# The entry of a two-layer graph kernel: weights' maxima, first norm and weight splits in another order

## What is computed

```python
h = relu(layernorm(x))                                   # 256 x 512
q, k, v = heads(h @ Wq + bq), heads(h @ Wk + bk), heads(h @ Wv + bv)   # 16 heads of 32
attn = softmax(where(adj == 0, -inf, q @ k.T / sqrt(32)))
x = x + (attn @ v) @ Wo + bo
h = relu(layernorm(x))
alpha = relu((h @ wq1) @ (h @ wk1).T) * (adj != 0)
x = x + softmax(alpha, axis=1) @ (h @ weight)
```

## Time and profile before

| | us |
|---|---|
| median of 3 runs | 1569.24 (1568.12 to 1569.25) |
| the profiled execution's own time | 1570.8 |
| its span in the trace | 1569.0 |
| mean granted TensorE clock in it | 0.992 of full |

### The profile page before, as it was taken

The page is one execution under the profiler, slowest core; times in us unless marked ns, Lnnn a source line. Parts: engine busy times, 40 slices in busy tenths (PEclk is TensorE's granted clock), DMA queues, the critical chain, the costliest instruction groups (busy, mean ns, idle before and its releaser), DMA issues.

```text
span 1569.0 us, 50846 instructions
## 1 busy us (share of the span) xinstructions
PE 1504.6 (96%) x16561; PEld 1106.7 (71%) x16561; DVE 1247.9 (80%) x4042; ACT 1128.3 (72%) x2477; POOL 1064.8 (68%) x1478
## 2 busy tenths in 40 slices
PE   2889999999999999999999999999999999999996
PEld 1557777777777777777777777777777777777753
DVE  6778888887887878788888878888887888888763
ACT  2567777777777777777777777777777777777761
POOL 2466767777677777767677776777776777777650
PEclk9999999999999999999999999999999999999998
DMA  7647777667667766666776766777676677767760
GB/s 241 135 95 132 133 163 160 152 136 152 138 138 166 160 144 143 144 136 148 166 157 141 152 140 134 154 160 159 135 158 136 133 161 160 153 135 159 125 119 16
DMA packets 656198, 226.28 MB, mean 144 GB/s; under 512 B 611488, under 2 KB 627872, under 8 KB 656160
## 3 DMA queue, kind: packets, MB, share of 16 engines
q1 hardware_dynamic: 636848, 188.57, 59.1%
q10 hardware_dynamic: 19312, 37.23, 8.5%
HBM read 57.94 MB, written 16.78 MB: 48 GB/s over the span
## 4 chain that ended last, share of the span: by engine, by line
POOL 35%; issue 34%; PE 22%; DVE 4%; ACT 2%; DMA 1%; POOLq 1%; SPq 0%; ACTq 0%; DVEq 0%
PE ring L408 18%; POOL wv_raw L1115 16%; POOL heads_out L1149 6%; POOL x L1172 4%; POOL keep L1181 3%; POOL far L1190 3%; POOL xa L1137 1%; PE score L464 1%; PE pv L483 1%; DMA turned<-wv_raw 1%; POOL newton L1133 1%; PE ring L518 1%; PE pv L485 0%; DVE wk_raw L864 0%; DVE tops L785 0%
## 5 line engine op out<-in xcount | busy, mean ns | idle before, releaser
L1115 POOL TENSOR_TENSOR wv_raw<-wk_raw,wv_raw 128x512 f16<-128x512 f32 x512 | 608.0, 1190 | 362.8 <-ACT wv_raw L638 358.5
L625 ACT ACTIVATE wk_raw<-wk_raw,least 128x256 f32<-128x256 f32 x1024 | 459.0, 497 | 6.8 <-DVE least L864 6.8
L864 DVE CUSTOM_DVE_ANT_0 wk_raw<-score,far,undo_score 128x256 f32<-128x256 f32 x1024 | 444.0, 478 | 7.1 <-issue 5.1
L638 ACT ACTIVATE wv_raw<-wk_raw 128x512 f16<-128x512 f32 x512 | 320.5, 626 | 8.6 <-issue 4.5
L483 PEld LDWEIGHTS pv<-val,turned 128*128 128x128 f16 x2048 | 149.7, 97 | 67.4 <-issue 43.9
L483 PE MATMUL pv<-val,turned 128*128 128x65 f16 x2048 | 185.9, 192 | 10.8 <-DMA turned<-wv_raw 7.0
L408 PE MATMUL ring<-wv_hi,h 128*128 128x256 f16 x1024 | 189.3, 273 | 0.0
L408 PE MATMUL ring<-h,wq_hi 128*128 128x256 f16 x1024 | 176.3, 274 | 7.6 <-DVE wk_lo L827 7.6
L1149 POOL TENSOR_TENSOR heads_out<-o_sum,o_rcp 128x64 f32<-128x64 f32 x512 | 153.0, 320 | 42.6 <-DVE o_sum L879 42.6
L485 PE MATMUL pv<-val,turned 128*128 128x33 f16 x2048 | 178.1, 179 | 0.0
L408 PE MATMUL ring<-h,wk_hi 128*128 128x256 f16 x1024 | 176.6, 274 | 0.0
(11 more groups left out here) (151 smaller groups left out, 3570.6 us busy)
## 6 DMA issues: line engine op xcount, KB each, us to landing
xin<-x_dram ACTq DMA_DIRECT2D x32, 512.0 KB, 3.8
out_dram<-xo SPq DMA_DIRECT2D x32, 512.0 KB, 3.7
xa<-x_dram ACTq DMA_DIRECT2D x31, 512.0 KB, 4.2
adj_in<-adj_dram SPq DMA_DIRECT2D x32, 256.0 KB, 2.9
turned<-wv_raw SPq DMA_TRANSPOSE x512, 3.2
adjt_in<-adj_t_dram SPq DMA_DIRECT2D x32, 256.0 KB, 3.1
wq_raw<-wq_dram SPq DMA_DIRECT2D x2, 512.0 KB, 7.0
wk_raw<-wk_dram SPq DMA_DIRECT2D x2, 512.0 KB, 8.6
```

The lines of the kernel that those rows point to most:

```text
L625: last = nc.scalar.activation(probs[:, at, q, :], probs[:, at, q, :], ACT.Exp, bias=least[:, at, q:q + 1], scale=-1.0)
L638: nc.scalar.activation(halves[:, at, :, 0, :], probs[:, at, :, :], ACT.Copy).then_inc(hi["p"], 1)
L864: last = nc.vector.tensor_tensor_reduce(out=probs[:, at, q, :], in0=score[u % GROUP][:, q * NODES:(q + 1) * NODES], in1=far[:, q, :], scal ...
L1115: nc.gpsimd.tensor_tensor(halves[:, at, :, 1, :], probs[:, at, :, :], halves[:, at, :, 0, :], ALU.subtract).then_inc(lo["p"], 1)
```

## The change

- **Loads.** SP issues wq right behind xa, then the biases, then wv; ACT's queue issues wk at the program's start.
- **Graph 0's norm.** VectorE does the refinement and the normalisation in place of POOL (three small instructions and two large ones in place of six and two).
- **Maxima first.** VectorE takes wq's and wk's maxima directly behind the low half of h, and the constants after them. `scaled` is raised as soon as the scales are there; `undo_score` and the two biases come behind it, with a semaphore of their own (`bias_ok`).
- **PE's start.** The first half of qk0 waits for wq's splits only. Eight float32 products of the identity with itself follow the first scale's products.
- **Values' scale.** Its rounding moves behind qk0's low half, its spreading behind graph 0's first scores.
- **Graph 1's norm.** Statistics in steps 12 and 13 of body(-1), root in 14, normalisation on POOL in 15, high half on ACT in step 1 of body 0, low halves in steps 2 and 3.
- **The nine jobs of body 0.** The spare places are now: h2_0 turn (scales of wo and w1), h2_1 merge 0, g0 spread, g1 merge 1, hw0 merge 2, al merge 3, hw1 turn (wm's scale), av0 spread, av1 bias product. ACT copies a merged tile out of its bank (`merged_copy`), VectorE takes the maximum of the copy. wo's maxima stand in step 15 of body(-1), w1's in steps 3 and 4 of body 0.
- **Splits.** wo in steps 8 and 9 of body 0, w1 in 10 and 11, wm in step 15 and in step 1 of body 1.

The code of bodies 2 and later is the same.

```diff
 STATS1, ROOT1, NORM1, LATE_MASK = (8, 9), 10, 12, 5
 XA_STEP, SCALE_STEP = 5, 6
+STATS1_FIRST, ROOT1_FIRST, NORM1_FIRST, HIGH1_FIRST, LOW1_FIRST = (12, 13), 14, 15, 1, (2, 3)
 HIGH1_STEP, LOW1_STEPS, TURN1_STEP = 14, (0, 2), 6
 VAR2 = 4
...
+JOBS = {"h2_0": "turn", "h2_1": 0, "g0": "spread", "g1": 1, "hw0": 2, "al": 3, "hw1": "turn",
+        "av0": "spread", "av1": "bias"}
+SPARE = [tile(name) for name in ORDER if tile(name) in JOBS]
+MERGES = [0, 1, 2, 3, "bias"]
+WARM = 8
...
-SPLIT_TURN = ("wq", "wk", "wv", "wo", "wm", "w1")
-TOP_STEP = 5
-LAST_SCALE_STEP = step_of(SPARE[-1])
-
-
-SPLIT_AT = {(0, 14): 6, (0, 15): 7, (1, 2): 8, (1, 3): 9, (1, 6): 10, (1, 7): 11}
-assert len(SPARE) == KT + 2 and TOP_STEP + 4 < LAST_SCALE_STEP
+TOP_AT = {(-1, 15): (("wo", 0), ("wo", 1)), (0, 3): (("w1", 0),), (0, 4): (("w1", 1),)}
+
+
+SPLIT_AT = {(0, 8): 6, (0, 9): 7, (0, 10): 8, (0, 11): 9, (0, 15): 10, (1, 1): 11}
...
             sp.dma_start(xa[:], x_v[0, :, :, :]).then_inc(xa_in, 16)
+            for half in range(2):
+                load_raw(sp, "wq", half)
             sp.dma_start(bias_q[:], bq).then_inc(small_in, 16)
             sp.dma_start(bias_k[:], bk).then_inc(small_in, 16)
             sp.dma_start(bias_v[:], bv).then_inc(small_in, 16)
             sp.dma_start(out_bias[:], bo.broadcast_to([P, DIM])).then_inc(small_in, 16)
-            for name in LOADS[:EARLY // 2]:
-                for half in range(2):
-                    load_raw(sp, name, half)
+            for half in range(2):
+                load_raw(sp, "wv", half)
...
+                dst, job = ring[BANK[SPARE[at]]], JOBS[SPARE[at]]
...
+                batch = 2 if at < 3 else 3
+                if job == "turn":
+                    turn_tops(batch, dst)
                     return
-                if at < KT:
-                    cols = slice(at * P, (at + 1) * P)
+                if job == "spread":
+                    spread_scale(batch, 2 if batch == 2 else 1, dst)
+                    return
...
-            WEIGHTS_BY = {("qk0", 0): (w_low, 4), ("v0", 0): (w_low, 6), ("wo0", 0): (w_low, 8),
-                          ("g0", 0): (w_low, 10), ("hw0", 0): (w_low, 12)}
+            WEIGHTS_BY = {("qk0a", 0): (w_low, 2), ("qk0b", 0): (w_low, 4), ("v0a", 0): (w_low, 6),
+                          ("wo0a", 0): (w_low, 8), ("g0", 0): (w_low, 12)}
...
@@ -594,16 +601,19 @@
                     if nxt and not cur and s == SCALE_STEP:
                         turn_tops(0, pv)
                         spread_scale(0, 2, pv)
-                    if nxt and not cur and s == step_of("qk0") - 1:
+                        for _ in range(WARM):
+                            nc.tensor.matmul(ring[1][:, 0:P], ident[:], ident[:], start=True,
+                                             stop=True)
+                    if nxt and not cur and s == step_of("qk0"):
                         turn_tops(1, pv)
-                    if nxt and not cur and s == step_of("qk0"):
-                        spread_scale(1, 1, pv)
                     if s in SCORE_STEPS:
                         g = SCORE_STEPS.index(s)
                         if g < 2 and nxt:
                             scores(g, t + 1)
                         elif g >= 2 and cur:
                             scores(g, t)
+                    if nxt and not cur and s == SCORE_STEPS[0]:
+                        spread_scale(1, 1, pv)
...
+            def merged_copy(name):
+                act.wait_ge(merged, MERGES.index(JOBS[name]) + 1)
+                nc.scalar.activation(raw["wm"][:, JOBS[name], :], ring[BANK[name]][:], ACT.Copy
+                                     ).then_inc(copied, 1)
...
+                    if isinstance(b, int) and b == 0 and k == 0:
+                        act.wait_ge(bias_ok, 1)
                     if k >= 2 or started(b - 1):
...
-                    if s == ROOT1 and later:
+                    if s == (ROOT1 if cur else ROOT1_FIRST) and later:
...
+                        elif cur and not prev and isinstance(JOBS.get(tile(name)), int) and not name.endswith("a"):
+                            merged_copy(tile(name))
...
-                    if nxt and not cur and s == step_of("qk0"):
+                    if nxt and not cur and s == SCORE_STEPS[0]:
                         act.wait_ge(scaled, 2)
                         for c in range(FIRST, EARLY):
                             split_high(c)
-                    if cur and not prev and s == LAST_SCALE_STEP:
-                        act.wait_ge(scaled, 3)
                     if cur and isinstance(t, int) and (t, s) in SPLIT_AT:
+                        act.wait_ge(scaled, 3 if SPLIT_AT[t, s] < 10 else 4)
                         split_high(SPLIT_AT[t, s])
-                    if s == HIGH1_STEP and later:
+                    if s == HIGH1_STEP and cur and later:
                         first_high(n + 1)
+                    if s == HIGH1_FIRST and cur and not prev:
+                        first_high(n)
                     if s == XA_STEP and later:
                         act.wait_ge(lo["h1"], count(n, QT, QT - 1))
                         act.dma_start(xa[:], x_v[n + 1, :, :, :]).then_inc(xa_in, 16)
+            for half in range(2):
+                load_raw(act, "wk", half)
...
-                src = ring[BANK[SPARE[at]]][:]
-                if at > KT:
-                    step(nc.vector.tensor_reduce(tops[:, 2, 0:1], most_merged[:], AX.X, ALU.max))
-                    find_scale(2, 3, 3, ring[BANK[SPARE[at]]])
+                bank, job = ring[BANK[SPARE[at]]], JOBS[SPARE[at]]
+                batch = 2 if at < 3 else 3
+                if job == "turn":
+                    round_tops(batch, 2 if batch == 2 else 1, bank)
                     nc.vector.sem_inc(merged_out, 1)
+                elif job == "spread" and batch == 2:
+                    take_scale(2, 3, 2, bank)
+                    nc.vector.sem_inc(merged_out, 1)
+                    nc.vector.sem_inc(scaled, 1)
                     step(nc.vector.tensor_tensor(undo_out[:], undo[:, 2:3], undo[:, 3:4],
                                                  ALU.mult))
                     step(nc.vector.tensor_scalar(undo_final[:], undo[:, 4:5], 1.0 / E_LIFT, None,
                                                  ALU.mult))
+                elif job == "spread":
+                    take_scale(3, 5, 1, bank)
+                    nc.vector.sem_inc(merged_out, 1)
                     nc.vector.sem_inc(scaled, 1)
-                    return
-                dve.wait_ge(merged, at + 1)
-                if at < KT:
-                    step(nc.vector.tensor_copy(raw["wm"][:, at, :], src))
-                    nc.vector.tensor_reduce(most_merged[:, at:at + 1], src, AX.X, ALU.max,
-                                            apply_absolute_value=True).then_inc(merged_out, 1)
+                elif job == "bias":
+                    dve.wait_ge(merged, MERGES.index(job) + 1)
+                    nc.vector.tensor_tensor(out_bias[:], bank[:], out_bias[:], ALU.add
+                                            ).then_inc(merged_out, 1)
                 else:
-                    nc.vector.tensor_tensor(out_bias[:], src, out_bias[:], ALU.add
-                                            ).then_inc(merged_out, 1)
+                    dve.wait_ge(copied, job + 1)
+                    step(nc.vector.tensor_reduce(most_merged[:, job:job + 1], raw["wm"][:, job, :],
+                                                 AX.X, ALU.max, apply_absolute_value=True))
+                    nc.vector.sem_inc(merged_out, 1)
+                    if job == KT - 1:
+                        step(nc.vector.tensor_reduce(top[:, 0:1], most_merged[:], AX.X, ALU.max))
+                        nc.vector.sem_inc(top_ok, 1)
...
+                    stats_at = STATS1 if cur else STATS1_FIRST
+                    if s in stats_at and later:
+                        first_stats(stats_at.index(s), n + 1)
+                    low_at = LOW1_STEPS if prev else LOW1_FIRST
+                    if s == low_at[0] and cur and nxt:
                         first_low(0, n)
+                    if isinstance(t, int) and (t, s) in TOP_AT:
+                        for name, half in TOP_AT[t, s]:
+                            raw_top(name, half, ("wo", "w1").index(name))
+                    if cur and not prev and s == 4:
+                        gather_tops(2)
...
-                    if nxt and not cur and s == step_of("qk0") - 1:
+                    if nxt and not cur and s == step_of("qk0"):
                         round_tops(1, 1, pv)
-                    if nxt and not cur and s == step_of("qk0"):
+                    if nxt and not cur and s == SCORE_STEPS[0]:
                         take_scale(1, 2, 1, pv)
                         nc.vector.sem_inc(scaled, 1)
...
+            y, a, c = rstd[0][:], newton[0][:, 1, :], newton[0][:, 2, :]
+            dve.wait_ge(rooted[0], 1)
```

(21 more changed lines are left out.)

47 lines of the change are left out of this document (18 added, 29 removed).

## The result

| | before | after |
|---|---|---|
| median, 8 runs each | 1567.78 (1566.38 to 1572.12) | 1571.53 (1570.33 to 1575.88) |
| ratio, with its 95% interval | | 1.0027 (1.0015 to 1.0039) |
| the profiled execution | 1570.8, span 1569.0 | 1571.63, span 1569.8 |

The changed kernel is slower, by 0.27%, where 0.4% faster was forecast. Its median lies 4.0 us above the upper end of the predicted range. The two profiled executions stand only 0.8 us apart, since that of before was itself above its median, so the place of the loss is read from the stages, not from the ends.

What follows compares the result with a forecast made beforehand. PE was taken to be full from body 2 on, with time lost before 153.2 us. Body 1 starting 2.3 us earlier and running 3.8 shorter gave 6.1 us, a median of 1563.1, range 1557.5 to 1567.5.

Steps and rivals of the forecast that it cites:

- The place of POOL's norm between the heads: Body 0: POOL's 3.7 us stand between the low halves of heads 1 and 2, 42.4 to 46.1; weigh 2 at 50.7.
- The wait of weigh 6 for sum 2: Body 0: weigh 6 waits until 65.9 for sum 2, which comes behind v1's low half and a mask.
- xa at 4.9: Entry: xa's landing moves by 0 to 1.3 us beside the weight loads; 0.7 taken, so 4.9 (4.18 before).
- Head 4's transposition runs beside the load of xin.: Body 0: started at 50.5 and taking 6.03 us, it gives weigh 4 at 56.5 (58.5), 2.0 us early.
- PE's clock: I take 0 for it.: Entry: if the eight products leave 1.2 GHz, scores start 1.2 later, weigh 0 by 0.8; taken as 0.
- One more stop of 3 us of PE before weigh 12.: Body 0: weigh 12 needs sum 5 behind the split of step 11, at 86.4 (86.0 in the old kernel).
- The stop at 92.49: Body 0: the old kernel's PE stop for the scales, claimed gone with the half clock behind it.
- the two wait for each other: Body 0 from 70.8 on: VectorE has 23 us of work, the same as PE's 23.6, so each waits for the other.
- the sum: Up to body 2: start at 147.1 in place of 153.2, 6.1 us earlier, so the median becomes 1563.1.
- the second: Body 0: the entry's gain is lost, only body 1's stays: 2 us, 1567; chance 0.19.
- the first: Body 0: VectorE and ACT don't hold PE; body 1 at 94.1, 12.9 us earlier, limit 1556; chance 0.25.
- half of it, 1559: Body 0: half the gain if VectorE and ACT don't hold PE, called plausible; all of it, 1556, the limit.

Runs made afterwards that it cites:

- Number 3: Changed kernel with body 0's load of xin issued by ACT in step 10 instead of step 4; ratio 1.0016 (1.0004-1.0027) to the kernel before.
- number 9: Changed kernel plus 36 f16 filler products behind weigh 1 of body 0, result unread; ratio 1.0039 (1.0024-1.0055) to the kernel before.
- 4: Changed kernel with w1's two splits and wm's first moved from body 0 to body 1; ratio 1.0014 (1.0004-1.0025) to the kernel before.
- 6: Changed kernel with the four splits of wo and w1 in steps 6 to 9 of body 0; ratio 1.0005 (0.9993-1.0016) to the kernel before.
- 11: Changed kernel with graph 1's norm, jobs and values' scale back, xin in step 10, wo and w1 splits early; ratio 0.9973 (0.9961-0.9984) to before.
- 15: 11 with v1's and v0's second halves ahead of the scale spreads in steps 5 and 15 of body 0; 1561.45 us, ratio 0.9952 (0.9939-0.9966) to before.
- number 7: Kernel before with the entry's part of the change alone; values' scale, graph 1's norm, jobs and splits old; ratio 0.9998 (0.9986-1.0010) to before.
- 1: Changed kernel with graph 1's first norm back in its old steps; ratio 1.0000 (0.9990-1.0009) to the kernel before.
- number 10: Changed kernel without the eight float32 products of the identity; ratio 1.0042 (1.0025-1.0058) to the kernel before.
- 2: Changed kernel with v1's second half ahead of merge 0 in step 5 of body 0; ratio 1.0031 (1.0020-1.0042) to the kernel before.
- 5: Changed kernel with the nine jobs in old order and wm's first split in step 0 of body 1; ratio 1.0004 (0.9992-1.0017) to before.
- 13: Changed kernel with VectorE, not ACT, copying the merged tiles and taking their maximum from the bank; ratio 1.0053 (1.0039-1.0066) to the kernel before.

## Why the prediction was wrong, step by step

| point | predicted | measured | what the step to it adds to the error |
|---|---|---|---|
| xa landed | 4.9 | 5.5 | +0.6 |
| first split on ACT | 21.0 | 21.56 | 0 |
| first scores | 30.7 or 31.9 | 32.0 | -0.5 by the second |
| body 0 (weigh 0) | 44.0 | 45.4 | +1.3 |
| weigh 2 | 50.7 | 52.2 | +0.1 |
| weigh 3 | 52.1 | 56.1 | **+2.5** |
| weigh 4 | 56.5 | 60.9 | +0.4 |
| weigh 6 | 65.9 | 70.6 | +0.3 |
| weigh 12 | 86.4 | 93.2 | **+2.2** |
| body 1 | 100.1 | 109.4 | **+2.5** |
| body 2 | 147.1 | 156.8 | +0.4 |
| body 3 | 193.3 | 204.1 | +1.1 |

**Right.** The entry's mechanisms, to 1.4 us of the start of body 0: the low half of h at 12.0 (11.4), the maxima to 16.9 (16.4), the split at 21.56, qk0's first half without a wait for wk. The place of POOL's norm between the heads. The wait of weigh 6 for sum 2 (2.7 forecast, 2.29 measured), and that the entry's lead would be gone by then, though it had turned into 5.1 us of delay (70.6 for 65.5). Body 1: 47.0 forecast, 47.36 measured.

**"xa at 4.9".** It took 4.79 us from its issue, alone 3.43: 1.36 more, the upper bound of the prediction, not its middle. The Trainium skill ("DMA: Bandwidth & Descriptors", Issuing engines are not separate DMA queues) says that loads started by several engines interleave on the same DMA engines; this trace agrees in that xa landed later with ACT's two loads of wk beside it. SP's own wq stood right behind xa too, and no run parts the two.

**"Head 4's transposition runs beside the load of xin."** This is the first step that failed. The collision was in the sum, but with the head that suffered it before. The prediction had weigh 3 at 52.1 and so head 3's transposition begin 3.3 before it, at 48.8. It began at 50.41, 1.6 later, 1.4 of which are the entry's, and so just behind `xin` at 50.28. A step with 1.5 us of room to a 2.2 us penalty was taken at one value. `xin` had moved as well, from 51.90 to 50.28, with ACT's stream, while POOL's norm held the transpositions back. Number 3 measured the penalty: 5.6 us or 3.4.

**"PE's clock: I take 0 for it."** That sentence was on the entry alone, and nothing at all was put down for body 0, although the prediction listed stops there, before weigh 2, 6 and 12, as long as or longer than the one behind which the kernel before had lost the clock. The half clock made merge 1 and qk1 slow, 1.6 and 2.4 us (half of 3.22 and of 4.89 us busy). That is 4.0 of the 4.7 us that the steps from weigh 6 to body 1 were off. In the earlier stretch qk3's products took 4.4 us for 2.6, which is hidden in the table by the contention that I had put on head 4; that head's transposition, issued at 51.8, landed 5.0 us later and held nothing up. Over the body the clock cost 7.0 us where the kernel before paid 2.8.

**"One more stop of 3 us of PE before weigh 12."** It was two of 1.94, within 1 us of that size. "The stop at 92.49 [is] gone" was wrong: it came back at 90.86, with 1.94 us, for the scale of wm. On VectorE two splits, wm's last maximum and an eviction stood in a row before the sum.

**The judgement between the cases.** From weigh 4 on the prediction had VectorE and PE equal, 23 us each, "and the two wait for each other". Each wait on PE was then taken at its own length, with no term for what a stop costs behind it. With the 7.0 us of clock in place of 0 the sum would have come to 1570.1 at most, which is no gain. Of the rivals, the second (the entry's gain lost, 1567) names the right places but ends at no loss; the first, PE held by nobody, is refuted by 14.9 idle us. Its "half of it, 1559" isn't half of its own 12.9 us, which would give 1562.8, but a value between that rival and the forecast. Of the 1.3 us between the first scores and weigh 0, 1.1 are in the values' scale: rounding, spreading and taking it lasted from 31.92 to 33.83, where the sum had it done at 32.7.

**What stays open.** How much the clock costs by itself in the whole body; number 9 failed to show it. That the surplus in busy time, 4.2 us, is the clock's is worked out from the rows. Stops and half clock go together in the kernel after, and where the stop before weigh 12 went (4, 6, 11, 15), so did the stretch behind it. But the length of a stop doesn't decide it. In number 7 the clock stays full behind a stop of 2.24 us at 99.9, while number 11 has 6.8 us at half clock from 50.3 on and no stop over 1.15 ahead of it in body 0. And before weigh 6 PE stops 2.29 us in numbers 1 and 3 as in the kernel after, with the full clock behind it. Number 3's weigh 6 and merge 1:

```profile
68.31 0.19 PE L490 MATMUL pv<-val,turned 128*128 128x65 f16 x1 [2.29 <-DVE o_sum L911]
...
68.54 3.67 PE L455 MATMUL ring<-wq_t_raw,wk_t_raw 128*128 128x512 f32 x8
```

That pair prices one stretch by itself: from weigh 6 to weigh 7 it is 4.6 us in numbers 1 and 3 and 6.1 in the kernel after, and the 1.5 us are still there at weigh 12 (21.1 behind weigh 6 for 22.7). For the stretches behind weigh 2 and weigh 12 no two kernels have the same stop with and without them. What exactly brings the clock down isn't shown. Body 2 is 0.8 to 2.2 us longer than the 46.2 of the kernel before in all of these kernels but number 10 (46.1). In the kernel after PE waits in it for a transposition, 0.48 us before weigh 8 and 0.44 before the next body's first weigh, where the kernel before doesn't wait; what makes these late wasn't tried. And one split (87.61) took VectorE 2.13 us where the others take 1.28; nothing here says what held it.

## What to carry to other kernels

For each long stop of PE that a moved step makes, carry a price for the clock as a rival of its own: take the rows of the products that follow, at 1.2 GHz, and count half of their time (1.6 us by that count for the stretch behind weigh 6, 1.5 measured). It is an upper bound, since some stops here cost no clock. When one engine's stream is held back by a few microseconds, list the transfers that another engine issues at a fixed step and see what they now meet. And where a sum on another engine stands between an odd and an even step of PE, a long product belongs in just that gap: putting the merges back there gained 4.8 us by weigh 13, the whole entry 2.6.

## What the runs showed of the hardware

- A 512 KB load issued 0.13 us ahead of it on another engine's queue went with a transposing DMA of 5.6 us; without that load it took 3.4. In the entry two loads from ACT's queue beside xa, and two of SP's right behind it, went with 4.79 us for xa where it took 3.43 without them.
- Eight float32 products, PE busy for 3.76 us right ahead of a stretch of f16 products, did not bring the full clock forward: it came at 29.4 us with them and without. The Trainium skill ("TensorE: Matmul & The Clock Gate", The HAM clock gate) says that activity releases the gate; the trace agrees in that the full clock came behind the f16 products that begin at 25.4, and no run here shows that the eight float32 ones counted towards it.
- The clock can fall in one execution and not in another with the same instructions up to there. Eight executions (the kernel after and numbers 2, 3, 4, 5, 6, 9 and 13) share the entry's code. In 2, 3, 4 and 9 PE ran some 3.5 us at half clock from a point between 31.8 and 33.5 on, in the others it didn't, and weigh 0 came at 45.6 to 45.8 in place of 45.3 to 45.4. Number 3's first product of qk1, which took 0.38 us in the kernel after:

```profile
33.64 0.59 PE L412 MATMUL ring<-h,wq_hi 128*128 128x256 f16 x2
```

- The same loop code ran at 45.90 to 46.08 us a body in different executions, which over 28 bodies is more than most single edits here were worth. Where the half clock fell in the last stage mattered too: that stage, from the start of body 31, took 82.5 us in the profiled execution of before, with PE busy for 64.7 at a mean clock of 0.91, and 79.5 in that of after, with 61.6 at 0.95.
